# Stores of x1, x2, B and C issued from ScalarE, scans counted per half, another split of the products with C, and new slots, in a decoder layer of selective scan, cross attention and experts

## Time and profile before

| | before |
|---|---|
| median of three runs | 3113.24 us (3109.69 to 3125.89) |
| the profiled execution: its time / its span | 3102.2 us / 3100.4 us |
| mean granted TensorE clock | 0.904 |
| busy: TensorE, VectorE, ScalarE, GpSimd | 2543.5, 2235.6, 1779.8, 2116.9 us |
| matmuls: 14784; VectorE, ScalarE, GpSimd instructions | 3682, 3818, 1064 |
| chain that ended last, by engine | GpSimd 40%, TensorE 24%, issue 21%, ScalarE 6%, VectorE 4%, DMA 3% |

### The profile page before, as it was taken

How to read it: one execution, slowest core, us unless ns; L and a number is a source line. 1 busy time by engine, 2 the same in 40 slices (tenths; PEclk the granted TensorE clock), 3 DMA queues, 4 the chain that set the end, 5 groups by cost and what they waited for, 6 DMA issues and landing times.

```text
span 3100.4 us, 49625 instructions
## 1 busy us (share of the span) xinstructions
PE 2543.5 (82%) x14784; PEld 1745.3 (56%) x14784; DVE 2235.6 (72%) x3682; ACT 1779.8 (57%) x3818; POOL 2116.9 (68%) x1064
## 2 busy tenths in 40 slices
PE   4578888788888888888888888888887768999997
PEld 3345655565555656565666656565655444555554
DVE  2778888888888888888888888888888731232222
ACT  2566767766766667666666667776666532122221
POOL 3999888988888888888888888998889600000000
PEclk8888999989999888998888989999998867999999
DMA  3355555555555555555555555555555340123111
GB/s 124 113 136 142 146 145 148 160 150 152 157 155 151 147 143 151 151 152 142 148 147 145 150 147 150 149 156 152 149 144 153 87 138 7 57 66 105 57 58 27
DMA packets 258282, 399.83 MB, mean 129 GB/s; under 512 B 49921, under 2 KB 190593, under 8 KB 253922
## 3 DMA queue, kind: packets, MB, share of 16 engines
q1 hardware_dynamic: 254434, 394.56, 46.1%
q10 hardware_dynamic: 3584, 2.10, 0.3%
HBM read 301.06 MB, written 94.37 MB: 128 GB/s over the span
## 4 chain that ended last, share of the span: by engine, by line
POOL 40%; PE 24%; issue 21%; ACT 6%; DVE 4%; DMA 3%; SPq 2%; ACTq 0%; POOLq 0%; DVEq 0%
POOL arena L488 21%; POOL arena L498 17%; PE g_ps L1260 5%; PE a_ps L840 5%; PE d_ps L1278 5%; PE u_ps L1260 4%; POOL u L479 2%; ACT dA_ps L564 2%; DMA arena<-w_dram 1%; PE y_ps L840 1%; DVE arena L699 1%; PE f_ps L840 1%; SPq L366 1%; ACT probs L603 1%; PE d_ps L1283 1%
## 5 line engine op out<-in xcount | busy, mean ns | idle before, releaser
L488 POOL TENSOR_TENSOR arena<-arena 128x1024 f32<-128x1024 f32 x512 | 1209.2, 2362 | 283.6 <-DMA arena<-w_dram 271.9
L564 ACT ACTIVATE dA_ps<-arena,a_neg 128x252 f32<-128x252 f32 x2048 | 875.1, 464 | 418.5 <-DVE dA_ps L722 173.5
L699 DVE TENSOR_TENSOR_SCAN arena<-dA_ps,arena 128x512 f32<-128x512 f32 x704 | 845.5, 1215 | 219.0 <-ACT dA_ps L564 211.5
L498 POOL TENSOR_TENSOR arena<-arena 128x512 f32<-128x512 f32 (+1 forms) x512 | 859.7, 1679 | 17.3 <-DVE arena L699 17.3
L603 ACT ACTIVATE probs<-st_ps 128x512 f32<-128x512 f32 x512 | 299.3, 585 | 227.4 <-PE st_ps L840 224.8
L699 DVE TENSOR_TENSOR_SCAN dA_ps<-dA_ps,arena 128x512 f32<-128x512 f32 x320 | 390.2, 1219 | 3.3 <-ACT dA_ps L564 3.2
L772 DVE TENSOR_REDUCE mx<-s_ps 128x2 f32<-128x512 f32 x512 | 344.0, 672 | 59.6 <-PE s_ps L840 58.6
L840 PE MATMUL a_ps<-xT,w_conv 128*128 128x256 f32 x1536 | 380.3, 399 | 0.0
L840 PE MATMUL y_ps<-arena,sel 128*32 128x256 f32 x4096 | 274.1, 413 | 87.5 <-POOL arena L498 87.5
L840 PE MATMUL s_ps<-k_st,q_st 96*128 96x256 f32 x1024 | 289.2, 366 | 57.5 <-DVE mx L772 44.0
L840 PEld LDWEIGHTS a_ps<-xT,w_conv 128*128 128x128 f32 x1536 | 295.3, 198 | 56.9 <-issue 16.4
(11 more groups left out here) (107 smaller groups left out, 3473.5 us busy)
## 6 DMA issues: line engine op xcount, KB each, us to landing
arena<-delta_dram SPq DMA_DIRECT2D x512, 128.0 KB, 3.0
arena<-w_dram SPq DMA_DIRECT2D x512, 128.0 KB, 3.4
arena<-bc_dram SPq DMA_DIRECT2D x128, 256.0 KB, 5.5
q_st<-q_parts_dram SPq DMA_DIRECT2D x512, 64.0 KB
k_st<-k_parts_dram SPq DMA_DIRECT2D x512, 64.0 KB
delta_dram<-delta SPq DMA_DIRECT2D x32, 512.0 KB, 3.8
w_dram<-u SPq DMA_DIRECT2D x32, 512.0 KB, 5.8
k_parts_dram<-parts SPq DMA_DIRECT2D x32, 512.0 KB, 3.4
```

Of the source, the lines that this page charges most:

```text
L488: pool.tensor_tensor(dBu[:, n % NB], w_r[:, n // RP % 2, t % RP].unsqueeze(1).to_broadcast([P, QS, L]), bc_r[:, b.par, 0], ALU.mult).then_ ...
L498: pool.tensor_tensor(h[:, n % NH, states], h[:, n % NH, states], bc_r[:, b.par, 1, states], ALU.mult).then_inc(s_hC, 1)
L564: last = nc.scalar.activation(dA[n % NDA][:, q, :, 1:], delta_r[:, n // (2 * RP) % 2, t % RP].rearrange("p (c t) -> p c t", t=CH)[:, :, 1: ...
L699: nc.vector.tensor_tensor_scan(dst, decays, dBu[:, n % NB, 2 * half:2 * half + 2].rearrange("p q t -> p (q t)"), 0.0, ALU.mult, ALU.add).t ...
```

## The change

It does these things:

- `bc_store`, `store_x1` and `store_x2` are issued by ScalarE's queue instead of SyncE's (six DMAs a batch).
- `s_scan` becomes one semaphore for each half, so that both halves of a tile may be multiplied on VectorE.
- `HC_DVE` has eleven halves instead of ten: both of tiles 1, 6 and 10, and one each of 2, 3, 4, 8 and 9. GpSimd is left with eight full products and five half ones (before: six and ten).
- Every list is ordered anew and several slots are moved. On SyncE's queue replicate(0) goes from slot 15 to 13, replicate(1) from 3 to 0, replicate(2) from 7 to 3, replicate(3) from 11 to 9; w_store and delta_store from 13 and 12 to 11; load_x1 from 12 to 15, load_ctx from 14 to 12, load_x_tok from 2 to 1. On GpSimd w_piece goes from slot 12 to 13. On VectorE the maximum of a head (`row_max`) now comes behind the second scan of its slot and the products with C, and before `clear_starts`.

The diff; the parts left out only exchange lines of the same kind:

```diff
-HC_DVE = [(0, 1), (1, 1), (2, 1), (3, 1), (4, 1), (6, 1), (9, 1), (12, 1), (13, 1), (14, 1)]
+HC_DVE = [(1, 0), (1, 1), (2, 1), (3, 1), (4, 1), (6, 0), (6, 1), (8, 0), (9, 1), (10, 0), (10, 1)]
...
-O_SP = 11
-O_REP = 15
+O_SP = 10
+O_REP = 12
 O_SCAN = 17
 O_OUT = 36
-O_N1 = 39
+O_N1 = 40
 O_K = 31
 O_X1T = 40
 O_Q = 43
 O_V = 44
-O_LD = 45
+O_LD = 47
 O_S = 48
 O_MT = 52
 O_E = 57
 O_PV = 61
 O_ON = 63
-O_ONT = 77
+O_ONT = 78
 O_OF = 80
-O_N2 = 79
+O_N2 = 80
...
-        s_scan, s_scan_v = sem("scan_done"), sem("scan_done_in_psum")
+        s_scan, s_scan_v = [sem(f"half_{i}_scanned") for i in range(2)], sem("scan_done_in_psum")
...
-            def bc_store(b):
-                wait_all(sp, (s_xp, 1, b, 1), (s_bc[b.par], 32, b.back(2), 64 - 32 * b.par))
-                sp.dma_start(bc_dram[b.par], xp[RANK:RANK + 2 * NS]).then_inc(s_bc_st, 16)
...
-            def store_x1(b):
-                dst = of_batch(x1_dram, b)
-                wait_all(sp, (s_x1, TT, b, TT))
-                sp.dma_start(dst, xt[:]).then_inc(s_x1_st, 16)
...
-            def store_x2(b):
-
-                rows = x2_dram.rearrange("(a e n r) d -> n e r a d", a=TT, e=P // EC, r=EC)
-                rows = rows[bass.ds(b.c, 1)].rearrange("n e r a d -> (n e) r a d")
-                wait_all(sp, (s_x2, TT, b, TT))
-                for q in range(X2_DMAS):
-                    sp.dma_start(rows[q], r2[EC * q:EC * (q + 1)]).then_inc(s_x2_st, 16)
             run_steps([
+                (O_REP + 1, replicate(0)),
+                (O_XP + 2, bc_load),
+                (O_Q + 1, store_parts(q_dram, s_q_hi, s_q_lo, s_q_dram)),
+                (O_REP + 13, replicate(3)),
+                (O_SP + 1, w_store),
+                (O_SP + 1, delta_store),
+                (O_OF - 1, load_x1),
+                (O_REP + 7, replicate(2)),
+                (O_K - 3, load_ctx),
                 (0, load_x),
-                (O_K - 1, load_ctx),
-                (O_SP + 1, delta_store),
-                (O_XP + 3, bc_load),
-                (O_SP + 2, w_store),
-                *[(O_REP + 4 * part, replicate(part)) for part in range(NU // 4)],
-                (O_OUT - 2, load_x_tok),
-                (O_K + 1, store_parts(k_dram, s_k_hi, s_k_lo, s_k_dram)),
-                (O_N1 + 1, store_x1),
-                (O_XP + 1, bc_store),
-                (O_Q + 1, store_parts(q_dram, s_q_hi, s_q_lo, s_q_dram)),
-                *[(O_LD + HG * gr, load_stack(gr)) for gr in range(NG)],
-                (O_OF - 4, load_x1),
-                (O_N2 + 2, store_x2),
                 (O_S, load_experts),
+                (O_REP + 4, replicate(1)),
+                (O_K + 4, store_parts(k_dram, s_k_hi, s_k_lo, s_k_dram)),
+                *[(O_LD + HG * gr - 2, load_stack(gr)) for gr in range(NG)],
+                (O_OUT - 3, load_x_tok),
...
-                        pool.wait_ge(s_scan, 2 * (n - NB) + 2)
+                        pool.wait_ge(s_scan[1], n - NB + 1)
...
-                    pool.wait_ge(s_scan, 2 * n + halves[-1] + 1)
+                    pool.wait_ge(s_scan[halves[-1]], n + 1)
...
-                (O_SP + 1, w_piece),
+                (O_SP + 3, w_piece),
...
-                        act.wait_ge(s_scan, n - NDA + 1)
+                        act.wait_ge(s_scan[(n - NDA) % 2], (n - NDA) // 2 + 1)
...
+            def bc_store(b):
+                wait_all(act, (s_xp, 1, b, 1), (s_bc[b.par], 32, b.back(2), 64 - 32 * b.par))
+                act.dma_start(bc_dram[b.par], xp[RANK:RANK + 2 * NS]).then_inc(s_bc_st, 16)
+
+            def store_x1(b):
+                dst = of_batch(x1_dram, b)
+                wait_all(act, (s_x1, TT, b, TT))
+                act.dma_start(dst, xt[:]).then_inc(s_x1_st, 16)
+
+            def store_x2(b):
+
+                rows = x2_dram.rearrange("(a e n r) d -> n e r a d", a=TT, e=P // EC, r=EC)
+                rows = rows[bass.ds(b.c, 1)].rearrange("n e r a d -> (n e) r a d")
+                wait_all(act, (s_x2, TT, b, TT))
+                for q in range(X2_DMAS):
+                    act.dma_start(rows[q], r2[EC * q:EC * (q + 1)]).then_inc(s_x2_st, 16)
...
             run_steps([
-                (O_SP, softplus),
+                (O_N1 - 2, norm(0, xt, s_mv1, s_ln1, s_x1)),
+                (O_Q + 1, high(s_q_mm, s_q_hi, s_k_dram, 0)),
                 *[(O_CONV + 4 * half + 3, conv_evac(half)) for half in range(2)],
+                (O_SP + 1, softplus),
+                (O_K + 1, high(s_k_mm, s_k_hi, s_q_dram, 1)),
+                *[(O_MT + HG * gr + 2, max_store(gr)) for gr in range(NG)],
                 *[(O_GATE + 4 * half + 1, gate_evac(half)) for half in range(2)],
-                (O_K + 1, high(s_k_mm, s_k_hi, s_q_dram, 1)),
+                *[(O_SCAN + t - 1, decay(t, 0)) for t in range(NU)],
+                (O_N2 + 2, store_x2),
+                *[(O_PV + HG * gr + 1, oT_evac(gr)) for gr in range(NG)],
+                (O_ONT - 1, onT_evac),
+                *[(O_MT + HG * gr + 3, max_load(gr)) for gr in range(NG)],
                 (O_XP + 1, xp_evac),
-                (O_Q + 1, high(s_q_mm, s_q_hi, s_k_dram, 0)),
-                (O_ONT + 1, onT_evac),
-                *[(O_SCAN + t - 1, decay(t, 0)) for t in range(NU)],
-                *[(O_PV + HG * gr + 1, oT_evac(gr)) for gr in range(NG)],
                 *[(O_E + hd, softmax_exp(hd)) for hd in range(H)],
+                (O_N1 - 1, store_x1),
+                (O_XP + 1, bc_store),
+                *[(O_SCAN + t - 1, decay(t, 1)) for t in range(NU)],
                 (O_SILU, silu),
-                *[(O_MT + HG * gr + 1, max_store(gr)) for gr in range(NG)],
-                *[(O_MT + HG * gr + 2, max_load(gr)) for gr in range(NG)],
-                *[(O_SCAN + t - 1, decay(t, 1)) for t in range(NU)],
-                (O_N2 + 2, norm(1, r2, s_mv2, s_ln2, s_x2)),
-                (O_N1 - 1, norm(0, xt, s_mv1, s_ln1, s_x1)),
+                (O_N2 + 1, norm(1, r2, s_mv2, s_ln2, s_x2)),
...
-                    nc.vector.memset(state[:, :, :, 0:1], 0.0).then_inc(s_scan, 1)
+                    nc.vector.memset(state[:, :, :, 0:1], 0.0).then_inc(s_scan[half], 1)
...
             run_steps([
-                (O_X1T + 1, x1T_evac),
+                (O_X1T + 2, x1T_evac),
                 *[(O_SCAN + t, scan(t, 0)) for t in range(NU)],
+                *[(O_SCAN + 4 * m + 6, gating(m)) for m in range(ND)],
+                (O_OF + 1, residual(1, r2, s_of_mm, a_ps, s_r2, s_st2, s_mv2, s_ln2, s_x1_ld)),
+                (O_K + 1, low(s_k_hi, s_k_lo)),
+                (O_V + 1, v_evac),
+                (O_OUT + 1, residual(0, xt, s_out_mm, a_ps, s_r1, s_st1, s_mv1, s_ln1, s_xtok)),
                 *[(O_MT + HG * gr + 1, max_parts(gr)) for gr in range(NG)],
-                (O_K + 1, low(s_k_hi, s_k_lo)),
-                (O_OUT + 1, residual(0, xt, s_out_mm, a_ps, s_r1, s_st1, s_mv1, s_ln1, s_xtok)),
-                *[(O_SCAN + 4 * m + 7, gating(m)) for m in range(ND)],
-                (O_V + 1, v_evac),
-                (O_OF + 1, residual(1, r2, s_of_mm, a_ps, s_r2, s_st2, s_mv2, s_ln2, s_x1_ld)),
                 *[(O_ON + HG * gr + 1, head_norm(gr)) for gr in range(NG)],
-                (O_Q + 1, low(s_q_hi, s_q_lo)),
-                *[(O_S + hd + 1, row_max(hd)) for hd in range(H)],
                 *[(O_SCAN + t, scan(t, 1)) for t in range(NU)],
                 *[(O_SCAN + t, hC_piece(t, half)) for t, half in HC_DVE],
+                *[(O_S + hd + 1, row_max(hd)) for hd in range(H)],
+                (O_Q + 1, low(s_q_hi, s_q_lo)),
...
             run_steps([
                 *[(O_E + hd, scores_T(hd)) for hd in range(H)],
+                *[(O_PV + HG * gr, pv(gr)) for gr in range(NG)],
+                *[(O_V, v_proj(tt)) for tt in range(TT)],
+                *[(O_OF, attn_out(tt)) for tt in range(TT)],
+                *[(O_CONV + 2 * m, conv(m)) for m in range(ND)],
+                *[(O_OUT, out_proj(tt)) for tt in range(TT)],
+                *[(O_DT, dt_proj(m)) for m in range(ND)],
                 *[(O_K, k_proj(m)) for m in range(KD)],
                 (O_X1T, transpose(xt, s_x1, TT, s_x1T_mm, s_x1T, bank_a, a_ps)),
-                *[(O_OUT, out_proj(tt)) for tt in range(TT)],
                 *[(O_Q, q_proj(m)) for m in range(KD)],
-                (O_ONT, transpose(on, s_on, NG, s_onT_mm, s_onT, bank_a, a_ps)),
-                *[(O_PV + HG * gr, pv(gr)) for gr in range(NG)],
-                *[(O_CONV + 2 * m, conv(m)) for m in range(ND)],
-                *[(O_OF, attn_out(tt)) for tt in range(TT)],
                 *[(O_ON + HG * gr, head_transpose(gr)) for gr in range(NG)],
-                *[(O_DT, dt_proj(m)) for m in range(ND)],
-                *[(O_GATE + 4 * (m // 2), gate_proj(m)) for m in range(ND)],
-                *[(O_V, v_proj(tt)) for tt in range(TT)],
-                (O_XP, x_proj),
-                *[(O_S + hd, scores(hd)) for hd in range(H)],
```

(4 more changed lines are left out.)

## The result

The changed kernel takes 2879.13 us, the median of four runs (2874.31 to 2886.43), against 3118.48 us for the kernel before, now also the median of four. The ratio is 0.9235 with a 95% interval of 0.9201 to 0.9270: 7.6% faster. I had forecast 2980 us with a range from 2900 to 3075, so the direction was right, and the gain is nearly twice what I gave it (239 us for 133), outside the range. Executions in a slower state of the chip, with a lower granted clock, are left out; that is one of four in the last run of the series that starts from the kernel before (3358.7 us at a clock of 0.721).

The account below looks back on a forecast made before the run. GpSimd, waiting for late parts, bounds the kernel; afterwards VectorE does: 67.0 + 0.5 + 1.4 + 1.3 = 70.2 us against 74.4, times 31 steps, saves 130 us: 2972, plus 0.35% 2982, said 2980; range 2900 to 3075.

Parts of the forecast that it names:

- GpSimd's step: In the middle steps GpSimd works 65.6 us and waits 9.4 and 0.6, so it sets the whole 75.6 us step.
- the order of the queue as the cause of late parts: SyncE's queue: part 1's DMAs stood behind store_x2 and load_x_tok, buffer free at 1241.1, issue from 1257.15; GpSimd waits 9.4 us a step.
- VectorE's floor: VectorE's occupied time, 66.4 us a step before, rises by 0.6 for products with C to 67.0 and becomes the bound.
- The step that the floor was set against: The forecast step of 70.2 us was compared with the 74.4 us mean step, saving 4.2 us in each of 31 steps.
- The waits left, 3.2 us: Waits added to VectorE's 67.0 us a step: 0.5 for part 0, 1.4 for load_x1, 1.3 for the others.
- rival D: Slower, 12%: chain behind w_store 1.4 times as slow, load_x1 lands at 26 us, residual(1) waits 8.5 us; 3190 us.
- my signs: Checks named ahead, such as GpSimd's w_dram wait under 60 us and SyncE's longest wait being for GpSimd's product at w_store.
- New orders: New orders on TensorE and VectorE: effect unknown, bounded by the 9.1 us a step of waits they should remove, and as much again.
- load_ctx, "0": SyncE's queue: load_ctx moves ahead and no longer costs TensorE its wait; TensorE has slack, so 0.
- Products with C: GpSimd's eight full and five half products instead of six and ten take 1.5 us a step less; VectorE gains 0.6.
- The profile against the median: The profiled execution lay 0.35% below the median, so 0.35% was added to 2972 us, giving 2982.
- Rival A: Denser still, 12%: load waits caused nearly all others, so VectorE's 67.0 plus 0.7 gives a 67.7 us step; 2905 us.

## Why the prediction was wrong, by its own steps

**GpSimd's step, and the order of the queue as the cause of late parts: right.** Parts early alone are worth 2.3%, late again they cost 460 us. But I had put the queue's 19 us a batch at the stores forward as what weighs more; the runs with the stores moved alone, and put back alone, show 0. A wait taken out of an in-order queue only brings the queue to its next wait. What frees a load is to stand ahead of the waits.

**VectorE's floor, 67.0 us: this is the term that failed.** It is occupied 64.5 us. 2.5 x 31 = 78 of the 101 us between 2980 and 2879 are this term. The value that I started from, 66.4, was not at fault (the 24 steps give 66.7). I added one product at its old price of 0.95 us, took off 0.3 for the pairs, and left the other ten as they were: +0.6 where the runs show -2.2. I had read that the maximum moves between product and clearing and priced it only as a bank that comes free late (0 to 4.8 us of loss). It also fills the drains: 1.9 us less in the kernel before, 1.4 more when put back.

That this floor is what the step hangs on was part of the same term, and it does not hold either. With the maxima moved alone VectorE is occupied 1.9 us less and the kernel is 2% slower; with the maxima last it is occupied 1.0 us more and the kernel is 0.7% faster. GpSimd is occupied as long as VectorE (64.5 us), and the waits that one engine leaves in the other count as well.

**The step that the floor was set against:** 70.2 us was built from a stretch with steps of 75.5 us and then taken off the mean of all 31, 74.4, which has the four short steps at the start in it. The middle steps of the changed kernel are 67.6 us, its mean is 67.2: 0.3 x 31, some 10 us of the miss.

**The waits left, 3.2 us: their sum was right (3.0), its parts were not.** Part 0 cost GpSimd 0.3 us a step for my 0.5, load_x1 0.2 for my 1.4: w_store landed in 3.5 us and not in the 5.8 of the earlier trace rows, and load_x1, issued just when I had said, in 3.3 and not in 4.7. The others are 2.6 for my 1.3. So rival D's chain was never near. Of my signs one failed: the queue's longest wait in `mixers` is not for GpSimd's product at w_store (83.5 us) but for a buffer of the parts to be free.

```profile
SPq L356 <- ACT dA_ps L547: 423.1, 64, 15.4
```

**New orders, "unknown", taken as 0: wrong.** In the changed kernel they are worth 188 us together. Part of that is in the floor above (1.4 us a step for VectorE's order). I could have said from the lists that TensorE's scores go last exactly where the maxima go later.

**load_ctx, "0": wrong as a price by itself.** Its move is what allows part 0's; without it the same kernel loses 238 us. I had costed each move by its own wait before and not by what is now put in front of it.

**Products with C: the size on GpSimd was right** (1.4 us less with the new split than the old; I said 1.5), but its worth depends on the rest: 80 us gained or some 60 lost by the slots around it.

**The profile against the median:** I added 0.35%; this time the profiled execution (2879.4 us) is the median. 8 us of the miss (2972 for 2980).

Rival A came nearest with 2905 us at 12%, and that is luck: its step of 67.7 us is my floor of 67.0 and 0.7 of waits, where the runs show 64.5 and 3.0. Two errors cancel. What stays open: from 2990 us (queue and orders in the old slots) to the changed kernel's 2879 there are ScalarE's order, the moved slots of pieces on ScalarE, VectorE and TensorE, GpSimd's w_piece a slot later, load_x1, load_x_tok and the store of k's parts at other places of the queue, and the split with them. VectorE's waits for decays are 4.6 us a step there and 1.5 here; which of these moves does it no run shows.

## What to carry to other kernels

In a program where several in-order queues feed each other, price a move by everything that it is put in front of or behind, and look first for loads that stand behind a wait although their buffer is free; taking one wait out of a queue helps only if the next wait is not reached in its place. An engine's occupied time is not a constant of its work: filling the time between two dependent instructions with an independent one took 1 to 2 us of 66 off VectorE here, and even so a buffer or bank that comes free sooner can be worth more. Parts of such a change do not add up: test the whole and then each part from both sides.

## What the runs showed that I had not expected

- What a product costs on VectorE depends on its neighbours: 1.12 us from a scan's start to a product of another bank, 1.25 to a product of its own result; 0.60 us from a product to a maximum, 1.38 for two products and their clearing ahead of it where 1.19 did without. With eleven products a step that is 1 to 2 us.
- The mean granted TensorE clock (1 is the level of 2.4 GHz, the other level is 1.2) was 0.904 in the profiled run before and 0.938 after, 0.940 and 0.941 in the two fastest kernels, 0.869 to 0.882 in the three slowest. TensorE's occupied time went along, 63.0 us a step before and 58.6 after with the same 14784 matmuls. What the clock alone gives back no run separates, so a part of the gain may be the clock's; it does not set the time by itself, as the changed kernel with the old split has 0.941 and takes 2959.4 us.
- Three DMA issues on ScalarE's queue took 1.50 us, and the next activation started only behind them, after 1.28 us idle.
- A part of the change can cost more than the whole gains: the two slowest kernels, 3252.5 and 3339.7 us, each hold most of a change that as a whole is 7.6% faster.
